# Exp and scores by side in the last four slots of an attention pipeline

## The reference

```python
qh, kh, vh = proj(q, w_q, b_q), proj(k, w_k, b_k), proj(v, w_v, b_v)
scores = jnp.einsum('bhqd,bhkd->bhqk', qh, kh) / jnp.sqrt(D_K)
attn = jax.nn.softmax(scores, axis=-1)
out = jnp.einsum('bhqk,bhkd->bhqd', attn, vh)
```

## Time and profile before

| what | value |
|---|---|
| median of 3 runs | 1255.2 us (1250.92, 1255.2, 1255.43) |
| the profiled execution, its own time | 1252.54 us |
| its span, first to last instruction | 1250.8 us |
| what lies around the span | 1.7 us |
| TensorE busy, share of the span | 96% |
| VectorE | 74% |
| ScalarE | 62% |
| GpSimd | 31% |
| mean granted TensorE clock | 0.997 |

### The profile page before, as it was taken

The page is one execution under the profiler, slowest core; times in us unless marked ns, Lnnn a source line. Parts: engine busy times, 40 slices in busy tenths (PEclk is TensorE's granted clock), DMA queues, the critical chain, the costliest instruction groups (busy, mean ns, idle before and its releaser), DMA issues.

```text
span 1250.8 us, 20663 instructions
## 1 busy us (share of the span) xinstructions
PE 1204.7 (96%) x6998; PEld 599.3 (48%) x6998; DVE 922.8 (74%) x1867; ACT 778.6 (62%) x1090; POOL 381.9 (31%) x485
## 2 busy tenths in 40 slices
PE   8799999999999999999999999999999999999998
PEld 4443444545545445454554454454544444554443
DVE  3687886677777787777877778777877788678772
ACT  2355567675576665765667656667657666666664
POOL 5510113311522134420523206221153204430261
PEclk9999999999999999999999999999999999999999
DMA  7422122122222122222122222222122211212200
GB/s 251 118 57 65 44 52 69 44 52 57 56 69 63 36 66 57 61 65 54 48 63 70 56 56 69 47 66 52 40 57 68 52 39 42 67 28 52 52 19 18
DMA packets 56446, 74.99 MB, mean 60 GB/s; under 512 B 14720, under 2 KB 26520, under 8 KB 56088
## 3 DMA queue, kind: packets, MB, share of 16 engines
q1 hardware_dynamic: 55192, 72.96, 23.4%
q10 hardware_dynamic: 1152, 0.72, 0.2%
HBM read 18.06 MB, written 4.19 MB: 18 GB/s over the span
## 4 chain that ended last, share of the span: by engine, by line
PE 80%; DVE 7%; ACT 6%; issue 4%; SPq 1%; DMA 1%; ACTq 0%; POOL 0%; DVEq 0%
PE ms L480 36%; PE op L480 15%; PE sc L480 15%; PE mx L480 9%; DVE maxes L990 3%; ACT probs L801 3%; PE ms L590 2%; PE ms L531 2%; ACT moe L794 1%; SPq L427 1%; PE ms L585 1%; DMA w_ident<-in_ident 1%; ACT k_parts L737 1%; DVE q_parts L900 0%; DVE heads L963 0%
## 5 line engine op out<-in xcount | busy, mean ns | idle before, releaser
L990 DVE TENSOR_REDUCE maxes<-mx 128x1 f32<-128x512 f32 x1024 | 657.5, 684 | 198.7 <-PE mx L480 196.9
L801 ACT ACTIVATE probs<-sc 128x1024 f32<-128x1024 f32 x512 | 525.0, 1025 | 369.1 <-PE sc L480 364.9
L1240 POOL TENSOR_TENSOR x<-x,moe 128x256 f32<-128x256 f32 x256 | 187.4, 732 | 646.3 <-ACT moe L794 624.7
L480 PE MATMUL op<-probs,v 128*32 128x512 f32 x2048 | 272.8, 605 | 0.4 <-ACT probs L801 0.3
L480 PE MATMUL sc<-qs,ks 50*128 50x512 f32 x1024 | 256.3, 497 | 13.8 <-ACT probs L801 12.8
L480 PEld LDWEIGHTS sc<-qs,ks 50*128 50x128 f32 x1024 | 95.3, 183 | 307.1 <-ACT probs L801 234.8
L480 PE MATMUL mx<-ks,qs 48*128 48x512 f32 x1024 | 209.5, 404 | 8.9 <-DVE maxes L990 6.7
L794 ACT ACTIVATE moe<-ms,comb 128x256 f32<-128x256 f32 x256 | 107.1, 473 | 20.1 <-PE ms L480 20.1
L480 PEld LDWEIGHTS mx<-ks,qs 48*128 48x128 f32 x1024 | 97.4, 187 | 22.4 <-DVE maxes L990 16.6
L480 PE MATMUL ms<-we_hi,x2T_hi 128*128 128x512 f32 x256 | 92.8, 443 | 3.2 <-DVE q_parts L900 1.0
L480 PEld LDWEIGHTS op<-probs,v 128*32 128x32 f32 x2048 | 40.3, 108 | 93.7 <-issue 92.0
(11 more groups left out here) (155 smaller groups left out, 1302.4 us busy)
## 6 DMA issues: line engine op xcount, KB each, us to landing
ks<-k_parts SPq DMA_DIRECT2D x384, 64.0 KB, 2.3
qs<-q_parts SPq DMA_DIRECT2D x381, 64.0 KB, 2.2
xT_s<-in_xT SPq DMA_DIRECT2D x8, 512.0 KB, 3.8
x_s<-in_x SPq DMA_DIRECT2D x8, 512.0 KB, 4.2
out<-x SPq DMA_DIRECT2D x7, 512.0 KB, 3.1
x_s<-in_ctxT SPq DMA_DIRECT2D x6, 512.0 KB, 5.1
qs<-shift_r SPq DMA_DIRECT2D x128, 8.0 KB
x<-in_ctxT SPq DMA_DIRECT2D x2, 512.0 KB, 6.3
```

What stands on the lines that cost most here:

```text
L480: return nc.tensor.matmul(dst, lhsT, rhs, start=first, stop=last, skip_group_check=True)
L801: nc.scalar.activation(probs[:, (2 * s + h) % 3, :, :], sc[:], ACT.Exp).then_inc(exp_out, 1)
L990: nc.vector.tensor_reduce(maxes[:, g % 2, at:at + 1], mx[:, i % 3, :], AX_X, ALU.max).then_inc(max_out, 1)
L1240: nc.gpsimd.tensor_tensor(x2[:, n % 2, t, :], x2[:, n % 2, t, :], moe[:, k % 2, j * D:j * D + D], ALU.add).then_inc(acc, 1)
```

## The change

In the half slots 504 to 511 (`by_side`) the exp of 128 by 1024 becomes two of 128 by 512, one per side. Each has a semaphore of its own: the score product of side 0 raises `score_first`, the exp of side 0 raises `exp_first`, and the second ones raise `score` and `exp_out` as before. The score product of side 0 of the next half slot waits for the exp of side 0 alone, and that of side 1 for the exp of side 1. ScalarE's wait for `pv` is now ahead of its wait for the scores, in all the half slots. The filler products in half slots 505, 507 and 511 are dropped, those behind the last slot stay. `values` is unchanged: it stands behind both score products in TensorE's order, and it waits for both exps.

```diff
+def by_side(t):
+
+    return t >= 2 * (SLOTS * len(PHASES) - 4)
+
+
+def side_count(t):
+
+    return t + 1 - 2 * (SLOTS * len(PHASES) - 4)
...
+        score_first, exp_first = sem("score_first"), sem("exp_first")
...
             def scores(s, h):
 
                 g, kb = s // TB, s % TB
-                if 2 * s + h >= 1:
-                    pe.wait_ge(exp_out, 2 * s + h)
+                t = 2 * s + h
+                if t >= 1 and not by_side(t - 1):
+                    pe.wait_ge(exp_out, t)
                 if kb == 0 and h == 0:
                     pe.wait_ge(shift_in[g % 2], 16 * SIDES * (g // 2 + 1))
                 for side in range(SIDES):
                     at = 64 * side
+                    if by_side(t - 1):
+                        if side == 0:
+                            pe.wait_ge(exp_first, side_count(t - 1))
+                        else:
+                            pe.wait_ge(exp_out, t)
                     last = mm(sc[:, side, :],
                               ks[at:at + ROWS + SHIFT, g % RING, h, kb * P:kb * P + P].bitcast(F32R),
                               qs[at:at + ROWS + SHIFT, g % RING, h, :].bitcast(F32R), True, True)
+                    if side == 0 and by_side(t):
+                        last.then_inc(score_first, 1)
                 last.then_inc(score, 1)
...
-                    if s >= SLOTS * len(PHASES) - 4 and not UNITS[t - 1] + UNITS[t]:
+                    if s >= SLOTS * len(PHASES) and not UNITS[t - 1] + UNITS[t]:
                         pe.wait_ge(max_out, 4 * SLOTS * len(PHASES))
                         busy(1, 3 * P, mx[:, 0, :])
...
             def exps(s, h):
-                act.wait_ge(score, 2 * s + h + 1)
+                t = 2 * s + h
                 if s - 1 + h >= 1:
                     act.wait_ge(pv, s - 1 + h)
+                if by_side(t):
+                    act.wait_ge(score_first, side_count(t))
+                    nc.scalar.activation(probs[:, t % 3, 0, :], sc[:, 0, :], ACT.Exp).then_inc(exp_first, 1)
+                    act.wait_ge(score, t + 1)
+                    nc.scalar.activation(probs[:, t % 3, 1, :], sc[:, 1, :], ACT.Exp).then_inc(exp_out, 1)
+                    return
+                act.wait_ge(score, t + 1)
                 nc.scalar.activation(probs[:, (2 * s + h) % 3, :, :], sc[:], ACT.Exp).then_inc(exp_out, 1)
```

## The result

The changed kernel takes 1264.09 us (median of 4, 1263.21 to 1264.96) against 1253.27 us (median of 4, 1250.92 to 1255.43) before: ratio 1.0093, 95% interval 1.0074 to 1.0113. It is slower by 10.8 us, where -0.1 was forecast and 1250.6 to 1257.2 was the range.

The account below looks back on a forecast made before the run. TensorE was taken to bound the main part, a TensorE-ScalarE ring the last 12.96 us. Terms 0.07 + 0.02 - 0.27 + 0.07 = -0.11 us gave 1255.1 us from a median of 1255.2; range 1250.6 to 1257.2.

Parts of the forecast that it names:

- But for the order of two waits on ScalarE, both of which must be met anyway.: Main part, before half slot 504: the change was said to touch nothing else there, and the swap was given no cost.
- the cover I named: Main part: the exp is hidden, as TensorE is busy for 96% of the span and carries 80% of the wait chain.
- dropping them saves nothing: Half slots 505, 507, 511: fillers of 0.91 us each are hidden under an exp, so removing them gains nothing.
- rival 2: Tail: without the fillers TensorE's clock falls and the kernel is slower, 1256.4 or 1260 us; chance 0.12.
- early fall: Clock falling at 1232 us: each ring pays more for values and hand-overs, about +4 to +5 us, giving 1260.
- late fall: Clock falling at TensorE's last pause in the tail: values +0.9 and transposes +0.4 us, giving 1256.4.
- the last pause: TensorE's pause behind the scores of half slot 511: some 1.2 us instead of 0.28, where the last filler stood.
- 80% of reported busy: New tail: the values fill the ring, which leaves TensorE at about 80% of reported busy.
- The ring of the sides: Half slots 504 to 511: split exps make a slot 3.10 us instead of 3.22, as values hold TensorE; sum -0.11 us.
- Rival 1: Tail: the ring shortens to one side, 1.19 us per half slot, as values hold nothing up; -2.8 us, 1252.4; chance 0.07.
- Rival 3: Tail: the second exp starts so late that the sides run one after the other; +0.6 us, 1255.8; chance 0.06.
- The signs of being wrong: Tail: a slot of 2.4 us, a slot over 3.3 us, or a stretch with the clock under 1.00.

Follow-up runs that it names:

- run 10: Sides split, old order of waits, fillers of 505 and 507 dropped and that of 511 kept; 1255.74 against 1251.27 us before, ratio 1.0036.
- run 9: Sides split, old order of waits, filler of 511 dropped and those of 505 and 507 kept; 1250.74 against 1251.27 us before, ratio 1.0001.
- run 2: The changed kernel with the old wait order (scores first, then pv); 1255.50 us against 1253.05 before, ratio 1.0015.
- run 5: The kernel before with only the fillers of 505, 507 and 511 dropped; 1255.25 us against 1251.73, ratio 1.0033.
- run 6: The changed kernel without the wait for pv in the exps; 1254.09 us against 1251.73 before, ratio 1.0030.
- run 1: The kernel before with only the new wait order in the exps (pv ahead of score); 1260.52 us against 1253.05, ratio 1.0057.
- run 3: The changed kernel with its three fillers put back, sides split, new wait order; 1259.61 us against 1253.05 before, ratio 1.0045.
- run 4: The kernel before with only the sides split, old wait order and fillers kept; 1253.07 us against 1253.05, ratio 0.9989.
- run 7: The kernel before with the late wait written first in five other places on ScalarE and VectorE; 1253.16 us against 1251.73, ratio 1.0005.
- run 11: The kernel before with sides split, all fillers, old exp wait order, late wait first in five other places; 1250.89 us against 1251.27, ratio 0.9999.
- run 8: The changed kernel measured again, nothing altered; 1264.59 us against 1251.73 before, ratio 1.0111.

## Why the prediction was wrong, point by point

- *"But for the order of two waits on ScalarE, both of which must be met anyway."* This is the step that failed, priced at nothing. It makes each exp 0.06 us later. It reached the end because the cover I named was thin. From one pair of scores over the values to the next TensorE took 1.666 us (the median over the 208 slots from 16 to 223, from the scores of a first half to those of the second), and the exp's ring is 0.54 + 1.03 + 0.05 = 1.62. The slack was some 0.04. The earlier trace rows showed it, 0.06 us between 1216.51 and 1216.57, and I read them for the values alone. With 0.06 more the ring is 1.68, and the median became 1.679. Over these 208 slots this spacing grew by 3.6 us, and that from the second half to the next slot by 2.6 (sums 355.4 to 359.0 and 613.3 to 615.9). By which waits the second part came was not traced; the slack above explains only the first. With about 0.7 us between 448 and 504 and 0.2 to 0.5 in the tail the wait order is worth 7 to 8 us of the 10.8.
- *The fillers: "dropping them saves nothing".* Right as far as it went: with them the tail is 12.81, and at full clock without two of them (run 10) or without the third (run 9) 12.81 as well. But their worth was the clock, and I had it as rival 2, at 0.12. This is the second term that failed, put at nothing in the sum and measured at about 4 us. All five profiled executions without the three fillers (after, twice, and runs 2, 5 and 6) have a low stretch in the tail; of the six with all fillers (before, runs 1, 3, 4, 7 and 11) none has one in the tail. The price of an early fall, +4 to +5, was right: the change without and with fillers has a tail of 15.97 against 13.05 and an end of 12.0 against 10.7, +4.2 us. The +1.3 of a late fall has no trace that shows it: the one late fall, in run 9, began behind the last values and left the end 0.3 us longer. What I misjudged is which of the two comes: I gave most of the chance to the last pause, behind the scores of 511, but it fell 4 to 7 us into the tail, with single pauses of no more than about 1.1 us before it. I took 80% of reported busy as the new tail's and saw the danger in that last pause; the traces have 4.71 of 5.93 us (79%, after) and 2.55 of 3.89 (66%, run 5) ahead of the fall. The Trainium skill, "TensorE: Matmul & The Clock Gate", Part 1, says that activity releases the gate and that it closes again when the array idles. These traces agree in direction only: with less work the clock fell, but ahead of the fall no pause of TensorE in the tail was longer than 1.14 us (run 5).
- *The ring of the sides*: right in every term to within 0.02 us. Exp of 512 0.60, 0.49 apart, scores to values 0.43, values to scores 0.98 to 1.00, slot 3.10; tail 12.81 for 12.85. The values swallow the head start, and the effect of -0.15 us stands against a forecast of -0.11. Rival 1 didn't happen. The exps of 512 took 606 and 604 ns in the trace (means of 8 each in the changed kernel). The estimate of 613 ns by the rule of the Trainium skill, "ScalarE: Activation LUTs", section "What ACT_TABLE_LOAD costs", is a little above them.
- *Rival 3*, the second exp late by its wait: no. The second exp has one wait, in its own instruction, and the two start 0.48 to 0.49 apart in all eight half slots.
- *The signs of being wrong*: one of the three came, a clock under 1.00 in the tail. None of them looked at the main part, where most of the loss lay.
- *What cannot be settled here*: after and run 1 have another low stretch at 1177 us, of 6.8 us, which makes 448 to 504 longer by 3 us; runs 3 and 8, with the same wait order, have none, and runs 7, 9 and 11, with the old order, have one too. Ahead of it, from 1174.00 to 1177.90 in the trace after, TensorE was reported busy for 2.63 of 3.90 us. It comes in some executions and not in others, in either order of the waits. And slot 0 is reached anywhere between 63 and 70 us. Both widen the measurement; neither explains the result.

The sum of the stages: wait order 6.7 + 0.7 + 0.2 = 7.6 (the last from the tails of runs 3 and 4), clock 4.2, sides -0.2 make 11.6, against 10.8 and 12.9 us measured in the two comparisons. The medians of the single changes say the same: +7.5 (run 1), +3.5 (run 5) and 0.0 (run 4) make 11.0. The wait order is shown by an edit of two lines and by its reverse. That the missing fillers bring the fall is shown as a tendency, in executions with and without them; what decides it in a single execution stays open.

## What to carry to other kernels

Where an instruction waits for two semaphores, write the one that ends last first, and when a diff swaps two waits, look which of them becomes a separate instruction and ends late. Price it, as measured here, at 0.06 us for each time that it is the last to be met, and compare that with the slack, which is the difference between two rings and not the busy share. A filler whose time is hidden isn't free to remove: its price can be the clock of what follows, 4 us here, so look at how busy TensorE is left without it. And an edit that starts one half of a pair early gains nothing when the engine's next instruction in order must wait for the other half.

## What the runs showed that I had not expected

A semaphore wait as an instruction of its own took 17 ns on ScalarE, and when it was the last to be met some 45 ns passed between its end and the exp; met early it cost nothing that shows (main part 1035.5 us without it, 1035.0 and 1035.2 with it). And the clock fell to 0.50 without any long pause: in run 5 behind 3.9 us in which TensorE was reported busy for 2.55, with pauses of 1.14 us at most in the timeline.
